# Audio tower block on one core: the first loads reordered and split, x in two parts, and three small steps moved between VectorE and GpSimd

## The chip, the cores and the metric

One core of one Trainium2 chip. The time is device microseconds (us) of one execution of the whole program, from its inputs in device memory to the output there. Engines: TensorE (PE, with its weight loads PEld), VectorE (DVE), ScalarE (ACT), GpSimd (POOL), SyncE (SP, whose queue issues most transfers).

## What is computed

An audio of 32 rows by 1024 samples is cut into patches of 16, which gives 32 batches of 64 tokens. Per token:

```
h = silu(x_cat @ W_h.T + b_h) @ W_o.T + b_o + x_cat @ W_r.T + b_r      # 16 samples -> 512 -> 256
h = h + attention(layernorm(h)) @ W_out.T + b_out                      # 16 heads of 16, Wq Wk Wv 16x16
h = h + real(ifft(fft(layernorm(h)) @ (w_real + i w_imag))) + bias     # 256 x 256 mix
```

The layernorms have no weights; eps is 1e-5. All is float32 at the ends.

## The kernel before

The 2048 tokens are T = 16 tiles of 128 tokens. The engines' programs are written out by hand, each with its own order and its own waits on semaphores; an engine never passes a waiting instruction.

**Start (to about 17 us).** SyncE issues twenty loads one after the other (`L254` to `L272`): all of x (`xs`, sixteen pieces of 64 bytes for each partition), the biases `bh`, `br`, `bo`, the identity, `wo_raw` (W_o, 512 KB), three small `wqk`, tables of the attention, W_out and the frequency weights and tables (`freq_loaded` counts four, the last is `sine`). ScalarE's queue loads W_h and W_r. x and the weights W_h, W_r with their biases are each split into three bfloat16 terms: place a term, subtract it, place the rest, twice over. ScalarE places x (`L316`), VectorE subtracts (`L597`) and does all of the weights (`L587`, `L592`). TensorE turns the stacks of terms (`turn_stacks`, `L844`, and `L860`), and W_o in `L850`; ScalarE makes the leading part `wo_hi` (`L328`), VectorE the rest `wo_lo` (`L625`). TensorE then mixes tile 0 (`mix`, `L887` to `L893`), only after all of W_o is split. The small products for the attention weights (`L910`, `L911`), and W_out turned (`L916`) stand between tile 0 and tile 1, and their copies on VectorE (`L646` to `L655`) before tile 2.

**Stage 1 (17 to 46 us), a loop over tiles 2 to 15.** For each tile TensorE makes the hidden layer (`hidden`, `L874`), ScalarE its silu twice (`L335`, `L338`), VectorE the remainder `hid_lo` (`L631`), TensorE `mix`, ScalarE copies h (`L342`), VectorE takes its statistics (`L660`). GpSimd meanwhile waits for the frequency weights, folds them (`L464` to `L480`), adds a bias to each h (`residual_bias`, `L505`), and makes rstd (`L489`) and the normalized x (`L525`). VectorE waits for the first rstd in `mean_shift(0)` (`L673`, at t = 7), then keeps on with the value weights, the remainders, and the inputs of the first scores.

**Stage 2 (46 to 147 us), steps i = -1 to 16.** Step i holds work of several tiles. On TensorE: turn the h2 of tile i-1 (`turn_side`, `L974`), turn maxima and x, scores of tile i+2, scores of tile i+1 less their maxima, frequency mix of tile i-1 (`mix_freq`), projection of tile i (`project`), query, and the weighted values (`weigh`, `L985`, `L990`). On VectorE: `divide` (`L758` to `L771`), `variance2(i-1)` (`L792`, `L794`, and `L798`, which adds eps), `split_x`, four row maxima (`L744`), `split_max` (`L751` a cast, `L753` a subtraction with both inputs in SBUF, both only 16 wide), `residual` (`L788`, which makes h2), `finish` (y, `L780`). On GpSimd, in this order: `place_same` (`L497`), `split_side` (`L532`), `split_on` (`L538`), `inv_std2` (`L511`, a power), `add_bias` (h2b, `L517`), `residual_bias` of tile 10 + i while that is below 16, so in steps 0 to 5 (`L505`, hb_all), and `normalize` of tile i+4, so up to step 11 (`L525`, xh). The next `turn_side` on TensorE waits for `residual`.

In step 0 VectorE also makes `mix_lo` (`L699`, 128 x 512), for which the first projection waits (`L1017`).

## Time and profile before

| what | value |
|---|---|
| median of 3 runs | 148.73 us (148.66 to 148.88) |
| the profiled execution | 149.01 us, span from first to last instruction 147.2 us |
| granted TensorE clock | 1.000 of full speed |
| 0 to 7.5 us | PE idle, DVE busy 2.69, ACT 3.15, POOL 2.63 |
| 7.5 to 17 us | PE 9.24 of 9.50, DVE 6.73, POOL 3.20 |
| 17 to 45 us | PE 27.55 of 28.00, DVE 21.81, ACT 19.69, POOL 21.19 |
| 72 to 90 us | PE 17.18 of 18.00, DVE 16.55, ACT 11.41, POOL 13.85 |
| 90 to 129 us | PE 38.59 of 39.00, DVE 35.44, ACT 25.68, POOL 26.32 |
| 129 to 147.2 us | PE 13.66 of 18.20, DVE 12.05, POOL 7.84 |

The busy times overlap within an engine where instructions are pipelined, so a busy engine is not necessarily at its limit; what ended each wait tells more. In the timelines a row is one instruction or a run of like ones, and the bracket at its end tells how long the engine was idle before it and what released it.

### The profile page before, as it was taken

Reading aid. Unit: us, or ns where it says so; the run is one execution under the profiler, and the core shown is the slowest. Engines: PE = TensorE matmul, PEld = TensorE weight load, DVE = VectorE, ACT = ScalarE, POOL = GpSimd, SP = SyncE. Lnnn points to the kernel's source line nnn. Section 1 sums busy time; section 2 is a strip of 40 time slices with the busy share of each in tenths; the row PEclk is TensorE's granted clock in tenths of the full one; section 3 lists DMA queues with packets and bytes.
Section 4 is the critical chain, followed back from the end, with each engine's and each line's share of the span. In section 5 each row is a group of like instructions: output and inputs, shape, how many; then the busy total and the mean of one; then the engine's idle time right before and its main releaser. Section 6 shows DMA issues by size and latency. Waiting matters only on the chain.

```text
span 147.2 us, 6094 instructions
## 1 busy us (share of the span) xinstructions
PE 131.7 (89%) x2434; PEld 113.2 (77%) x2434; DVE 117.8 (80%) x350; ACT 88.1 (60%) x248; POOL 89.5 (61%) x160
## 2 busy tenths in 40 slices
PE   0099899999999999999899999999999999999872
PEld 0098899999988877868678787897898887887641
DVE  0747964879977469899998989989989889889671
ACT  4478475747969475837558476486495594663310
POOL 6020999998230015879786786865776766673351
PEclk9999999999999999999999999999999999999999
DMA  4567000021000001102112012022131131121102
GB/s 63 161 162 254 4 0 0 0 25 17 2 0 4 0 9 20 18 25 33 46 19 58 32 26 52 8 58 47 13 60 43 14 58 40 18 53 42 33 10 71
DMA packets 24492, 5.89 MB, mean 40 GB/s; under 512 B 20368, under 2 KB 24208, under 8 KB 24464
## 3 DMA queue, kind: packets, MB, share of 16 engines
q1 hardware_dynamic: 24176, 5.40, 17.3%
q8 instruction: 19, 0.31, 0.9%
q10 hardware_dynamic: 288, 0.10, 0.3%
q14 instruction: 9, 0.07, 0.2%
HBM read 2.35 MB, written 2.10 MB: 30 GB/s over the span
## 4 chain that ended last, share of the span: by engine, by line
PE 57%; DVE 19%; issue 12%; POOL 4%; ACT 3%; DMA 2%; POOLq 0%; DVEq 0%
PE bank L946 9%; PE bank L932 6%; PE bank L887 6%; DVE rowmax L744 5%; PE bank L1007 3%; PE bank L985 3%; PE bank L891 3%; PE bank L974 3%; PE bank L990 2%; PE bank L1028 2%; DMA xs<-in_x 2%; PE bank L959 2%; DVE hid_lo L631 2%; PE bank L874 2%; PE bank L1041 2%
## 5 line engine op out<-in xcount | busy, mean ns | idle before, releaser
L744 DVE TENSOR_REDUCE rowmax<-bank 128x4 f32<-128x256 f32 x64 | 22.7, 418 | 5.6 <-ACT pT L371 5.3
L371 ACT ACTIVATE pT<-bank 128x256 f32<-128x256 f32 x64 | 19.4, 390 | 2.5 <-PE bank L959 2.5
L497 POOL TENSOR_SCALAR xblk<-xh,parity_sb 128x128 f32<-128x128 f32 x32 | 11.5, 371 | 14.3 <-PE bank L990 14.3
L946 PE MATMUL bank<-qT,xzT 32*128 32x64 f32 x512 | 17.9, 276 | 0.0
L946 PEld LDWEIGHTS bank<-qT,xzT 32*128 32x128 f32 x512 | 15.7, 186 | 2.7 <-issue 2.7
L631 DVE TENSOR_TENSOR hid_lo<-hidT,hid_hi 128x512 fp32r<-128x512 f32 x16 | 12.2, 761 | 5.6 <-ACT hidT L338 5.5
L366 ACT ACTIVATE maxT<-bank 128x128 fp32r<-128x128 f32 x16 | 4.4, 277 | 19.8 <-PE bank L968 19.8
L532 POOL TENSOR_TENSOR side_lo<-sideT,side_hi 128x256 fp32r<-128x256 f32 x14 | 10.2, 730 | 9.5 <-ACT sideT L381 9.5
L538 POOL TENSOR_TENSOR on_lo<-onT,on_hi 128x256 fp32r<-128x256 f32 x14 | 10.3, 735 | 7.2 <-ACT on_hi L385 7.0
L505 POOL TENSOR_TENSOR hb_all<-h_all,bout_bc 128x256 f32<-128x256 f32 x16 | 12.4, 789 | 0.0
L361 ACT ACTIVATE qT<-bank 128x256 f32<-128x256 f32 x16 | 6.2, 388 | 9.9 <-PE bank L1052 9.9
L356 ACT ACTIVATE xzT<-bank,parity_sb 128x256 f32<-128x256 f32 x28 | 12.0, 498 | 0.0
L517 POOL TENSOR_TENSOR h2b<-h,fbias_bc 128x256 f32<-128x256 f32 x16 | 11.7, 731 | 0.0
L990 PEld LDWEIGHTS bank<-pT,xblk 128*32 128x32 f32 x512 | 9.5, 110 | 2.8
L511 POOL TENSOR_TENSOR rstd<-ve,half_neg 128x1 f32<-128x1 f32 x16 | 8.9, 554 | 4.4 <-DVE ve L798 4.4
L932 PE MATMUL bank<-xzT,qT 32*64 32x128 f32 x512 | 11.5, 280 | 0.0
L887 PE MATMUL bank<-wo_hi,hid_hi 128*128 128x256 f32 x64 | 11.4, 300 | 0.0
L335 ACT ACTIVATE hid_hi<-bank 128x512 fp32r<-128x512 f32 x16 | 9.6, 601 | 2.7 <-PE bank L874 2.7
L342 ACT ACTIVATE h_all<-bank 128x256 f32<-128x256 f32 x16 | 6.2, 385 | 8.2 <-PE bank L893 8.2
L525 POOL TENSOR_SCALAR xh<-h_all,rstd,shift 128x256 f32<-128x256 f32 x16 | 9.6, 600 | 1.2 <-issue 0.5
L891 PE MATMUL bank<-wo_hi,hid_lo 128*128 128x256 f32 x64 | 10.3, 282 | 0.0
L985 PE MATMUL bank<-pT,pair_ones_sb 128*32 128x256 f32 x128 | 10.2, 391 | 0.0
(152 smaller groups left out, 388.5 us busy)
## 6 DMA issues: line engine op xcount, KB each, us to landing
out<-y SPq DMA_DIRECT2D x16, 128.0 KB, 1.7
xblk<-xh SPq DMA_DIRECT2D x32, 32.0 KB, 2.2
wo_raw<-in_W_o SPq DMA_DIRECT2D x1, 512.0 KB, 3.7
wout_raw<-in_W_out SPq DMA_DIRECT2D x1, 256.0 KB, 3.0
fr<-in_wr SPq DMA_DIRECT2D x1, 256.0 KB, 4.3
fi<-in_wi SPq DMA_DIRECT2D x1, 256.0 KB, 4.3
xs<-in_x SPq DMA_DIRECT2D x1, 128.0 KB, 3.3
minus_raw<-in_minus_rows SPq DMA_DIRECT2D x1, 128.0 KB, 2.2
```

The source lines that it names most:

```text
L356: nc.scalar.activation(xzT[t % 3][:, :, e, :], bank[X_BANK][:, 0:D].rearrange("p (g k) -> p g k", k=TOK), ACT.Copy, scale=parity[:, e:e + ...
L371: nc.scalar.activation(pT[:, j, :], bank[j][:, D:2 * D], ACT.Exp).then_inc(exp_done, 1)
L505: nc.gpsimd.tensor_tensor(hb_all[:, t, :], h_all[:, t, :], bout_bc[:], ALU.add).then_inc(hb_done, 1)
L517: nc.gpsimd.tensor_tensor(h2b[t % 2][:], h2[t % 2][:], fbias_bc[:], ALU.add).then_inc(h2b_done, 1)
L631: nc.vector.tensor_tensor(hid_lo[:, par, :], hidT[:, par, :], hid_hi[:, par, :].bitcast(F32), ALU.subtract).then_inc(lo_done, 1)
L744: nc.vector.tensor_reduce(rowmax[:, j, :], bank[j][:, 0:D].rearrange("p (h k) -> p h k", k=TOK), AX_X, ALU.max).then_inc(max_done, 1)
L887: pe.matmul(bank[MIX_BANK[par]][:, 0:D], hid_hi[:, par, c * P:(c + 1) * P], w[:, c, :], start=(c == 0 and w is wo_hi), stop=False)
L891: pe.matmul(bank[MIX_BANK[par]][:, 0:D], hid_lo[:, par, c * P:(c + 1) * P], wo_hi[:, c, :], start=False, stop=False)
L932: last = pe.matmul(bank[j][TOK * b:TOK * b + TOK, half * P:(half + 1) * P], qT[t % 3][rows32, half, TOK * b:TOK * b + TOK], xzT[t % 3][row ...
L946: pe.matmul(bank[j][:, at0:at0 + TOK], xzT[t % 3][rows32, 2 * half + b, :, :].rearrange("p e k -> p (e k)"), qT[t % 3][rows32, half, TOK * ...
L985: pe.matmul(bank[PV_BANK][32 * j:32 * j + 32, D:2 * D], pair_ones[:], pT[:, j, :], start=True, stop=True)
L990: last = pe.matmul(bank[PV_BANK][32 * j:32 * j + 32, cols], xblk[t % 2][:, b, half * P + 32 * j:half * P + 32 * j + 32], pT[:, j, cols], s ...
```

## The change

- **Loads.** SyncE first loads four tiles of x (`HEAD` = 4), then b_h, W_o, W_r, b_r, b_o, the three small weights, the other twelve tiles of x, and the rest as before. The identity goes to ScalarE's queue behind W_h. b_h, W_h, W_r, the biases, and the two parts of x have semaphores of their own.
- **First four tiles of x.** ScalarE places them as before, GpSimd subtracts. VectorE does only W_h (four of the six columns of weights) before TensorE turns it; GpSimd then does W_r's terms.
- **Last twelve tiles of x.** GpSimd places and subtracts them after that; TensorE turns them at t = 2 and t = 3 of the loop, VectorE copies them at t = 3 and t = 4.
- **Tile 0.** W_o is turned in two halves; VectorE copies the leading part of the first, ScalarE that of the second. `mix(0)` takes its products in the order in which the operands arrive, with W_r's product last.
- **Later places in stage 1.** W_out is turned at t = 4, copied at t = 4 (VectorE); the small copies at t = 3, the score split at t = 5, the value weights at t = 5 instead of t = 4. Zeros for `xblk` and `max_terms` are set by VectorE.
- **Stage 2.** `mix_lo` is made by GpSimd in step 0 (waited for by `mix_freq(0)`, no longer by `project(0)`). eps is added by GpSimd ahead of the power, in `inv_std2`, for all 16 tiles; VectorE's `L798` goes.

```diff
+HEAD = 4
...
-        WO_BANK = (2, 3, 4, 5)
+        WO_BANK = (2, 3)
+        WR_BANK = 7
...
-            sp.dma_start(xs[:], x_tok).then_inc(x_loaded, 16)
-            sp.dma_start(bh[:], a["b_h"].rearrange("(p c) -> p c", p=P)).then_inc(b_loaded, 16)
-            sp.dma_start(br[:], a["b_r"].rearrange("(p c) -> p c", p=P)).then_inc(b_loaded, 16)
-            sp.dma_start(bo[:], a["b_o"].rearrange("(p c) -> p c", p=P)).then_inc(b_loaded, 16)
-            sp.dma_start(ident[:], a["identity"]).then_inc(ident_loaded, 16)
+            sp.dma_start(xs[:, 0:HEAD, :], x_tok[:, 0:HEAD, :]).then_inc(x_loaded, 16)
+            sp.dma_start(bh[:], a["b_h"].rearrange("(p c) -> p c", p=P)).then_inc(bh_loaded, 16)
             sp.dma_start(wo_raw[:], a["W_o"].rearrange("(c p) i -> p c i", p=P)).then_inc(wo_loaded, 16)
+            sp.dma_start(wf_raw[:, NC:, :], a["W_r"].rearrange("(p c) f -> p c f", p=P)).then_inc(wr_loaded, 16)
+            sp.dma_start(br[:], a["b_r"].rearrange("(p c) -> p c", p=P)).then_inc(br_loaded, 16)
+            sp.dma_start(bo[:], a["b_o"].rearrange("(p c) -> p c", p=P)).then_inc(br_loaded, 16)
             for i, name in enumerate(("Wq", "Wk", "Wv")):
-                sp.dma_start(wqk[:, i, :], a[name]).then_inc(att_loaded, 16)
+                sp.dma_start(wqk[:, i, :], a[name]).then_inc(wqk_loaded, 16)
+            sp.dma_start(xs[:, HEAD:, :], x_tok[:, HEAD:, :]).then_inc(x_late_loaded, 16)
...
-            sp.wait_ge(const_set, 8)
+            sp.wait_ge(zeros_set, 2)
...
-            act.dma_start(wf_raw[:, 0:NC, :], a["W_h"].rearrange("(p c) f -> p c f", p=P)).then_inc(w_loaded, 16)
-            act.dma_start(wf_raw[:, NC:, :], a["W_r"].rearrange("(p c) f -> p c f", p=P)).then_inc(w_loaded, 16)
-
+            act.dma_start(wf_raw[:, 0:NC, :], a["W_h"].rearrange("(p c) f -> p c f", p=P)).then_inc(wh_loaded, 16)
+            act.dma_start(ident[:], a["identity"]).then_inc(ident_loaded, 16)
...
-                nc.scalar.activation(x_slots[:, :, X_SLOTS[part], 0:PATCH],
-                                     src[:].unsqueeze(2).to_broadcast([P, T, n, PATCH]), ACT.Copy).then_inc(x_placed, 1)
-
+                nc.scalar.activation(x_slots[:, 0:HEAD, X_SLOTS[part], 0:PATCH],
+                                     src[:, 0:HEAD, :].unsqueeze(2).to_broadcast([P, HEAD, n, PATCH]),
+                                     ACT.Copy).then_inc(x_placed, 1)
...
+            act.wait_ge(x_turned, 1)
             for g in range(2):
-                act.wait_ge(x_turned, g + 1)
-                nc.scalar.activation(x_termsT[:, g * HID:(g + 1) * HID], bank16[6 + g][:, 0:HID],
+                nc.scalar.activation(x_termsT[:, g * D:(g + 1) * D], bank16[6][:, g * D:(g + 1) * D],
                                      ACT.Copy).then_inc(x_copied, 1)
...
-                if at(t, 0):
-                    wo_leading((2, 3))
+                if at(t, 1):
+                    act.wait_ge(wo_turned, 2)
+                    nc.scalar.activation(wo_hi[:, 2:4, :].rearrange("p c n -> p (c n)"), bank[WO_BANK[1]][:],
+                                         ACT.Copy).then_inc(wo_copied, 1)
...
-            wo_leading((0, 1))
...
             nc.gpsimd.memset(half_neg[:], -0.5).then_inc(const_set, 1)
             nc.gpsimd.memset(w_terms[:, :, STACK:P], 0.0).then_inc(const_set, 1)
-            nc.gpsimd.memset(x_terms[:, :, STACK:P], 0.0).then_inc(const_set, 1)
             nc.gpsimd.memset(x_slots[:, :, 0:3, PATCH], 1.0).then_inc(const_set, 1)
             nc.gpsimd.memset(x_slots[:, :, 3:TERMS, PATCH], 0.0).then_inc(const_set, 1)
-            for i in range(2):
-                nc.gpsimd.memset(xblk[i][:], 0.0).then_inc(const_set, 1)
-            nc.gpsimd.memset(max_terms[:].bitcast(F32), 0.0).then_inc(const_set, 1)
+            nc.gpsimd.memset(x_terms[:, :, STACK:P], 0.0).then_inc(const_set, 1)
...
+            def x_remainder(part, src):
+                pool.wait_ge(x_placed, part + 1)
+                nc.gpsimd.tensor_tensor(x_rest[part][:], src[:, 0:HEAD, :], x_slots[:, 0:HEAD, X_SLOTS[part].start, 0:PATCH],
+                                        ALU.subtract).then_inc(x_rest_set, 1)
+
+            def place_wr(part, src):
+                n = len(range(*W_SLOTS[part].indices(TERMS)))
+                nc.gpsimd.tensor_copy(w_slots[:, NC:, W_SLOTS[part], :],
+                                      src[:, NC:, :].unsqueeze(2).to_broadcast([P, HALF, n, TERM])).then_inc(wr_placed, 1)
...
+            def place_late(part, src):
+                n = X_SLOTS[part].stop - X_SLOTS[part].start
+                nc.gpsimd.tensor_copy(x_slots[:, HEAD:, X_SLOTS[part], 0:PATCH],
+                                      src.unsqueeze(2).to_broadcast([P, T - HEAD, n, PATCH])).then_inc(x_late_placed, 1)
...
+            def late_remainder(part, src):
+                pool.wait_ge(x_late_placed, part + 1)
...
+
+            x_remainder(0, xs)
             pool.wait_ge(ident_loaded, 16)
             nc.gpsimd.tensor_copy(ident16[:], ident[:]).then_inc(ident16_set, 1)
-
-
-            pool.wait_ge(att_loaded, 112)
+            pool.wait_ge(x_rest_set, 1)
+            x_remainder(1, x_rest[0])
+
+            pool.wait_ge(wr_set, 4)
+            place_wr(0, wb)
+            wr_remainder(0, wb)
+            place_wr(1, wb_rest[0])
+            wr_remainder(1, wb_rest[0])
+            place_wr(2, wb_rest[1])
...
+            pool.wait_ge(wqk_loaded, 48)
...
+            pool.wait_ge(x_late_loaded, 16)
+            place_late(0, xs[:, HEAD:, :])
+            late_remainder(0, xs[:, HEAD:, :])
+            place_late(1, x_late_rest[0][:])
+            late_remainder(1, x_late_rest[0][:])
+            place_late(2, x_late_rest[1][:])
...
-            pool.wait_ge(const_set, 8)
+            pool.wait_ge(zeros_set, 2)
...
             def inv_std2(t):
-                pool.wait_ge(ve2_done, t + 1)
+                pool.wait_ge(mv2_done, t + 1)
+                nc.gpsimd.tensor_scalar(ve2[:], mv2[:, 1:2], EPS, None, ALU.add).then_inc(ve2_done, 1)
                 if t >= 2:
                     pool.wait_ge(y_set, t - 1)
+                pool.wait_ge(ve2_done, t + 1)
                 nc.gpsimd.tensor_tensor(rstd2[t % 2][:], ve2[:], half_neg[:, 0:1], ALU.pow).then_inc(rstd2_done, 1)
...
+            def split_mix_weights():
+                pool.wait_ge(mix_led, 1)
+                pool.wait_ge(mix_kept, 1)
+                nc.gpsimd.tensor_tensor(mix_lo[:], mix_whole[:], mix_hi[:].bitcast(F32), ALU.subtract).then_inc(mix_split, 1)
...
             def step(i):
                 if i + 2 < T:
                     place_same(i + 2)
+                if i == 0:
+                    split_mix_weights()
...
+            for i in range(2):
+                nc.vector.memset(xblk[i][:], 0.0).then_inc(zeros_set, 1)
+            nc.vector.memset(max_terms[:].bitcast(F32), 0.0).then_inc(zeros_set, 1)
...
+            dve.wait_ge(wh_loaded, 16)
+            nc.vector.tensor_copy(wb[:, 0:NC, 0:PATCH], wf_raw[:, 0:NC, 0:PATCH]).then_inc(wh_set, 1)
+            nc.vector.tensor_reduce(wb[:, 0:NC, PATCH], wf_raw[:, 0:NC, PATCH:], AX_X, ALU.add).then_inc(wh_set, 1)
+            dve.wait_ge(bh_loaded, 16)
+            dve.wait_ge(wh_set, 2)
+            nc.vector.tensor_tensor(wb[:, 0:NC, PATCH], wb[:, 0:NC, PATCH], bh[:], ALU.add).then_inc(wh_set, 1)
+            dve.wait_ge(wh_set, 3)
+            place_wh(0, wb)
+            wh_remainder(0, wb)
+            place_wh(1, wb_rest[0])
+            wh_remainder(1, wb_rest[0])
+            place_wh(2, wb_rest[1])
+
+            dve.wait_ge(wr_loaded, 16)
+            nc.vector.tensor_copy(wb[:, NC:, 0:PATCH], wf_raw[:, NC:, 0:PATCH]).then_inc(wr_set, 1)
+            nc.vector.tensor_reduce(wb[:, NC:, PATCH], wf_raw[:, NC:, PATCH:], AX_X, ALU.add).then_inc(wr_set, 1)
+            dve.wait_ge(w_turned, 1)
+            nc.vector.tensor_copy(w_termsT[:, 0:HID], bank16[0][:, 0:HID]).then_inc(w_copied, 1)
+            dve.wait_ge(br_loaded, 32)
+            nc.vector.tensor_tensor(br[:], br[:], bo[:], ALU.add).then_inc(wr_set, 1)
+            dve.wait_ge(wr_set, 3)
+            nc.vector.tensor_tensor(wb[:, NC:, PATCH], wb[:, NC:, PATCH], br[:], ALU.add).then_inc(wr_set, 1)
...
+            dve.wait_ge(wo_turned, 1)
+            nc.vector.tensor_copy(wo_hi[:, 0:2, :].rearrange("p c n -> p (c n)"), bank[WO_BANK[0]][:]).then_inc(wo_led, 1)
...
+            remainder(0, 0)
+            for g in range(2):
+                wo_remainder(g)
+            dve.wait_ge(wr_turned, 1)
             nc.vector.tensor_copy(wr_termsT[:].rearrange("f (p c) -> f c p", c=HALF),
-                                  bank16[1][:, 0:D].rearrange("f (c p) -> f c p", c=HALF)).then_inc(w_copied, 1)
-            wo_remainder(range(NC))
-            remainder(0, 0)
+                                  bank16[WR_BANK][:, 0:D].rearrange("f (c p) -> f c p", c=HALF)).then_inc(wr_copied, 1)
             remainder(1, 1)
...
+            def copy_small():
+                dve.wait_ge(att_loaded, 64)
+                dve.wait_ge(small_done, 2)
...
+            def copy_wout():
+                for c in range(HALF):
...
+            def copy_late(g):
+                dve.wait_ge(x_late_turned, g + 1)
...
             for t in range(3, T):
+                if t == 3:
+                    copy_late(0)
                 remainder(t, t % 2)
+                if t == 3:
+                    copy_small()
+                if t == 4:
+                    copy_late(1)
                 h_stats(t - 2)
+                if t == 4:
+                    copy_wout()
+                if t == 5:
+                    split_score()
...
                 nc.vector.bn_stats(stats2[:], h2[t % 2][:]).then_inc(stats2_done, 1)
                 dve.wait_ge(stats2_done, t + 1)
+                if t >= 1:
+                    dve.wait_ge(ve2_done, t)
                 nc.vector.bn_aggr(mv2[:], stats2[:]).then_inc(mv2_done, 1)
-                dve.wait_ge(mv2_done, t + 1)
-                if t >= 1:
-                    dve.wait_ge(rstd2_done, t)
-                nc.vector.tensor_scalar(ve2[:], mv2[:, 1:2], EPS, None, ALU.add).then_inc(ve2_done, 1)
...
-                if i == 0:
-                    split_mix_weights()
...
-            dve.wait_ge(const_set, 8)
+            dve.wait_ge(zeros_set, 3)
...
+                if at(t, 0):
+                    pe.wait_ge(x_copied, 2)
+                    pe.wait_ge(wo_led, 1)
+                    leading(t, par, wo_hi, (0, 1))
+                    pe.wait_ge(wo_copied, 1)
+                    leading(t, par, wo_hi, (2, 3))
+                    pe.wait_ge(lo_done, 1)
+                    remaining(t, par)
+                    pe.wait_ge(wo_split, 2)
+                    leading(t, par, wo_lo, range(NC))
+                    pe.wait_ge(wr_copied, 1)
...
             hidden(0, 0)
-            turn_wo((2, 3))
-            pe.wait_ge(w_copied, 2)
+            pe.wait_ge(ident_loaded, 16)
+            pe.wait_ge(wo_loaded, 16)
+            turn_wo(0)
             hidden(1, 1)
-            pe.wait_ge(x_copied, 2)
-            turn_stacks(8, 8, 7)
-            mix(0, 0)
-            hidden(2, 0)
-
+            turn_wo(1)
             pe.wait_ge(reps_set, 2)
             pe.matmul(bank[4][:, 0:P], wrep[:, 0, :], wrep[:, 1, :], start=True, stop=True).then_inc(small_done, 1)
             pe.matmul(bank[4][:, P:2 * P], erep[:], wrep[:, 2, :], start=True, stop=True).then_inc(small_done, 1)
-
-            pe.wait_ge(wout_loaded, 16)
+            pe.wait_ge(wr_placed, 3)
             for c in range(HALF):
-                for k in range(HALF):
-                    last = pe.transpose(bank[2 + c][:, k * P:(k + 1) * P], wout_raw[:, k, c * P:(c + 1) * P], ident[:])
-                last.then_inc(wout_turned, 1)
+                last = pe.transpose(bank16[WR_BANK][:, c * P:(c + 1) * P], w_terms[:, NC + c, :], ident16[:])
+            last.then_inc(wr_turned, 1)
+            mix(0, 0)
+            hidden(2, 0)
             mix(1, 1)
...
+                if t == 0:
+                    pe.wait_ge(mix_split, 1)
...
-                    pe.wait_ge(mixw_copied, 1)
+                    pe.wait_ge(mix_kept, 1)
...
+                if t == 2:
+                    pe.wait_ge(x_late_placed, 3)
+                    turn_stacks(HEAD, HEAD, 7, x_late_turned)
+                if t == 3:
+                    pe.wait_ge(x_late_copied, 1)
+                    turn_stacks(2 * HEAD, 2 * HEAD, 7, x_late_turned)
+                if t == 4:
+                    turn_wout()
+                if t == 7:
+                    pe.wait_ge(x_late_copied, 2)
...
-                if t == 4:
+                if t == 5:
+                    pe.wait_ge(wout_copied, HALF)
                     value_weights()
```

## Rows read from the trace of the kernel before

**Rows 1.** The page: busy time, share of the span and instructions of each engine.
```profile
PE 131.7 (89%) x2434; PEld 113.2 (77%) x2434; DVE 117.8 (80%) x350; ACT 88.1 (60%) x248; POOL 89.5 (61%) x160
```

**Rows 2.** TensorE's instructions in order of time: start us, us, work, [idle before].
```profile
7.56 0.58 PE L860 MATMUL bank<-ident,w_terms 128*128 128x128 bf16 x4 [7.56 <-DVE w_terms L587]
...
17.18 0.40 PE L874 MATMUL bank<-x_termsT,w_termsT 128*128 128x128 bf16 x4 [0.39 <-DVE woutT L655]
```

**Rows 3.** SyncE's queue in order of time: start us, us to issue, transfer.
```profile
1.22 1.51 SPq L255 DMA_DIRECT2D bh<-in_b_h  x1
...
10.49 0.43 SPq L271 DMA_DIRECT2D sine_sb<-in_sine  x1
```

**Rows 4.** GpSimd in order of time, 14 to 28 us.
```profile
14.88 0.74 POOL L464 TENSOR_TENSOR rows<-fr 128x256 f32<-128x256 f32 x1 [4.17 <-DMA sine_sb<-in_sine]
...
19.64 0.39 POOL L472 COPY rows<-fi 1x256 f32<-1x256 f32 x1
...
20.11 0.46 POOL L475 TENSOR_TENSOR cols<-rows 128x127 f32<-128x127 f32 x1
...
20.51 0.19 POOL L476 COPY cols<-rows 128x1 f32<-128x1 f32 x1
...
27.33 1.41 POOL L489 TENSOR_TENSOR rstd<-ve,half_neg 128x4 f32<-128x4 f32 x1
```

**Rows 5.** VectorE in order of time, 28 to 33 us.
```profile
28.78 0.69 DVE L673 SCALAR_TENSOR_TENSOR shift<-mv,rstd 128x4 f32<-128x4 f32 x1 [0.60 <-POOL rstd L489]
...
32.35 0.69 DVE L631 TENSOR_TENSOR hid_lo<-hidT,hid_hi 128x512 fp32r<-128x512 f32 x1 [0.75 <-ACT hidT L338]
```

**Rows 6.** Chain of waits, 15 to 58 us: start us, us, the work.
```profile
40.72 0.43 DVE x_lo L711
```

**Rows 7.** All engines in order of time, 80 to 89 us (step 4; last row step 5).
```profile
80.01 0.74 POOL L538 TENSOR_TENSOR on_lo<-onT,on_hi 128x256 fp32r<-128x256 f32 x1 [0.57 <-ACT on_hi L385]
...
81.23 0.73 POOL L517 TENSOR_TENSOR h2b<-h,fbias_bc 128x256 f32<-128x256 f32 x1
...
81.86 0.17 DVE L751 CAST max_terms<-rowmax 128x16 fp32r<-128x16 f32 x1
...
81.92 0.73 POOL L505 TENSOR_TENSOR hb_all<-h_all,bout_bc 128x256 f32<-128x256 f32 x1
...
82.07 0.61 DVE L753 TENSOR_TENSOR max_terms<-rowmax,max_terms 128x16 fp32r<-128x16 f32 x1
...
82.61 0.41 DVE L788 TENSOR_TENSOR h<-bank,hb_all 128x256 f32<-128x256 f32 x1
...
88.52 0.41 DVE L788 TENSOR_TENSOR h<-bank,hb_all 128x256 f32<-128x256 f32 x1
```

**Rows 8.** VectorE and GpSimd at the end of step 2, in order of time.
```profile
69.70 0.45 DVE L751 CAST max_terms<-rowmax 128x16 fp32r<-128x16 f32 x1
...
70.08 0.73 POOL L505 TENSOR_TENSOR hb_all<-h_all,bout_bc 128x256 f32<-128x256 f32 x1
...
70.18 0.66 DVE L753 TENSOR_TENSOR max_terms<-rowmax,max_terms 128x16 fp32r<-128x16 f32 x1
```

**Rows 9.** VectorE and GpSimd in steps 6 and 9, in order of time.
```profile
93.78 0.55 POOL L525 TENSOR_SCALAR xh<-h_all,rstd,shift 128x256 f32<-128x256 f32 x1
...
93.90 0.45 DVE L753 TENSOR_TENSOR max_terms<-rowmax,max_terms 128x16 fp32r<-128x16 f32 x1
...
110.93 0.55 POOL L525 TENSOR_SCALAR xh<-h_all,rstd,shift 128x256 f32<-128x256 f32 x1
...
111.01 0.19 DVE L753 TENSOR_TENSOR max_terms<-rowmax,max_terms 128x16 fp32r<-128x16 f32 x1
```

**Rows 10.** TensorE's `turn_side` of steps 5 and 12, in order of time.
```profile
89.08 0.41 PE L974 MATMUL bank<-ident,h 128*128 128x128 f32 x2 [0.27 <-DVE h L788]
...
128.88 0.44 PE L974 MATMUL bank<-ident,h 128*128 128x128 f32 x2
```

**Rows 11.** GpSimd at step 0, in order of time.
```profile
55.95 0.73 POOL L538 TENSOR_TENSOR on_lo<-onT,on_hi 128x256 fp32r<-128x256 f32 x1 [1.36 <-ACT on_hi L385]
```

185 lines of the change are left out of this document (83 added, 102 removed).

## The prediction

> **What bounds the kernel now.** I read the page first: PE is busy for 89% of the span, DVE for 80%, POOL for 61% [rows 1]. So three engines are near enough to a limit that a share decides nothing, and I went by stage. Start: PE does nothing before 7.56 us, where it has waited for the last term of the weights, and its loop begins with hidden(3) at 17.18 [rows 2]. SP's queue shows why the inputs are late: b_h took 1.51 us to issue, against 0.43 for others, behind the many small pieces of x; the last frequency table was issued only at 10.49 [rows 3]. GpSimd waited for that table until 14.88, then worked without a gap worth the name to its first rstd at 27.33 [rows 4]. VectorE waits for this rstd: its shift starts at 28.78 and takes 0.69 instead of some 0.15, as it stands behind GpSimd. After the value weights it idles 0.75, then runs from 32.35 [rows 5] as the chain itself to 40.72 [rows 6]. So GpSimd and then VectorE, not PE, set the later part of stage 1.
>
> Stage 2 has the important pattern. In step 4 GpSimd goes on_lo, power, h2b, hb_all back to back. VectorE's `L753`, a subtraction of 16 columns, starts at 82.07 and lasts 0.61; it ends at 82.68, just behind the end of hb_all (81.92 + 0.73 = 82.65). h2 follows at 82.61, and everything on PE follows h2 [rows 7]. Step 2 shows the pattern for a GpSimd that is a little later: the cast `L751` is held to 70.15, and `L753`, at 70.18, finds hb_all begun at 70.08 and is held to 70.84 [rows 8]. So in steps 1 to 5 the period (88.52 - 82.61 = 5.91 for h2 [rows 7]) is the time of GpSimd's chain, though the chain of waits names VectorE and "issue". In steps 6 and on there is no hb_all. In step 6 `L753`, 0.12 behind the start of xh, is held to 94.35; in step 9, only 0.08 behind it, it slips in and takes 0.19 [rows 9]. From step 5 to step 12, `turn_side` moves from 89.08 to 128.88, seven periods of 5.69 [rows 10], close to what PE needs.
>
> **The change, part by part.** The sum is made on the profiled execution (149.01); I carry its differences over to the median, 148.73, which lies 0.28 lower.
>
> *Loads.* A quarter of x leaves a quarter of b_h's stall of 1.51 - 0.43 = 1.08: 0.27. b_h and what follows comes about 0.8 earlier, and W_o goes third instead of sixth. Behind the other twelve tiles the next issue pays the stall back (0.75 x 1.08 = 0.81), and there is one more load (W_r joins, the late x joins, the identity leaves), 0.47. The last table thus moves by -0.81 + 0.81 + 0.47 = +0.47 at most; if the stall isn't proportional, by nothing. I take +0.3: GpSimd's rows start near 15.2. The late x on GpSimd is five operations; at 0.46 for 127 columns [rows 4] and 192 to 576 columns each, some 3.3 us, and the W_r part some 2. They end near 14, in the wait before 14.88, so they are hidden; if that cover failed, stage 1 would be later by the overrun.
>
> *PE's start.* With b_h and W_h early and x of four tiles, its first transpose comes near 5.2 instead of 7.56. PE then waits for GpSimd's small copies, which stand behind the W_r terms (near 9.8), so the loop gains less. Into the loop move turns of x and W_out of 1.0 us together. I put PE ahead by 1.5 us at t = 7. There it stops: `turn_x(0)` at t = 8 needs GpSimd's xh, and VectorE needs GpSimd's rstd. The extra copies on VectorE at t = 3 to 5 lie before that wait. Behind it only the idle 0.75 before 32.35 [rows 5] can go, with its 0.06 of hand-over, as silu(9) is now early: 0.81. Less the 0.3 of the table: **-0.5**. Bounds: 0 (the table is later, or a copy stalls PE) and -1.5 (all of PE's lead).
>
> *Mix of tile 0 by arrival* costs nothing of its own: the same thirteen products. Its gain is inside PE's start.
>
> *mix_lo on GpSimd.* 512 columns at twice 0.73 is 1.4 us; GpSimd idles 1.36 before on_lo at step 0 [rows 11]. Zero; without that gap it would be 1.4 in one step.
>
> *eps on GpSimd.* VectorE loses a tiny operation in each step. In step 4 it stood idle before the maxima anyway, so I count no gain. GpSimd gains one ahead of its power. The nearest row is the copy of one column: 0.19, and it frees its successor after some 0.18. The power must then wait for it; a wait of GpSimd for itself shows as 0.08 (19.64 + 0.39 to 20.11) [rows 4]. So the GpSimd chain is 0.26 longer; bounds 0.15 (no wait seen) and 0.45. Queued behind it are h2b, hb_all, xh. In step 4, h2b would end at 82.22, the cast be held to it, and `L753` come 0.10 behind hb_all's start, as in step 2: held, and h2 0.26 later. Five steps, 1 to 5: 5 x 0.26 = **+1.3** (0.75 to 2.2).
>
> *Steps 6 to 12.* In step 6 h2b ends at 94.05, the cast at 94.08, `L753` starts at 94.11, that is 0.07 behind xh at 94.04. In step 9 0.08 was enough to slip in [rows 9]. Then it ends at 94.29 instead of 94.35. Steps where it was not held lose 0.1 or so, those where it was held gain 0.06: **0** (-0.2 to +0.3).
>
> At that point a rule speaks against the row. The Trainium skill ("SBUF — State Buffer", Who interferes with whom) says that of a VectorE instruction with two SBUF inputs and a GpSimd instruction that reads SBUF, whichever issues first keeps the shared port to its end. By that rule xh, 0.07 earlier, wins, and the sum is that of the second rival below.
>
> *Tail.* In the last two tiles GpSimd waits for VectorE's eps. Added 0.26, removed an operation of VectorE: between 0 and 0.26 each, I take 0.1 each: **+0.2**.
>
> Sum: -0.5 + 1.3 + 0 + 0.2 = +1.0. 148.73 + 1.0 = 149.7.
>
> **The rivals.** *(1) Faster: the lead of the start survives and eps is hidden.* If the small addition is done while the port is VectorE's, or `L753` gets the port between h2b and hb_all, steps 1 to 5 cost nothing. That leaves 148.73 - 0.5 = 148.2, and down to 147.2 if PE's whole 1.5 is kept. It decides where h2 in step 4 comes less than 0.1 later after `turn_side`. For it: the start has much to win. Against it: step 2's row, and that GpSimd, not PE, is ahead of VectorE at t = 7. *(2) `L753` loses to xh.* Then in step 6 it ends at 94.04 + 0.55 + 0.03 = 94.62 instead of 94.35: +0.27 in four steps that were held before, and some +0.4 in three that weren't: +2.3, in all 152.0. For it: hb_all held a subtraction 0.10 behind. Against it: the 0.08 of step 9. *(3) Both ends meet.* The full 1.5 of the start and +1.3 +0.2 of stage 2: 148.7, no change. The gain of the start would have to pass the wait for rstd, for which the freq loads must land 0.5 us earlier, not later.
>
> That mix_lo or the W_r terms hold up PE I count into (2)'s side: both have cover, and both would be some tenths.
>
> **How the numbers follow.** A measurement of this kernel can tell about 0.2%, 0.3 us, from no change. Forecast 0.45 (its own range 149.1 to 150.5), rival (1) 0.25, (2) 0.20, (3) 0.10. Slower: 0.45 + 0.20 = 0.65; faster 0.25; same 0.10. The range takes in all of the forecast, (3), the upper half of (1) and most of (2): 148.0 to 152.0.
>
> **What would show it.** PE's first transpose near 5.2 and hidden(3) near 14.7. GpSimd's rows at 15.0 to 15.4, its first rstd at 27.4 to 27.8. VectorE's hid_lo of tile 9 near 31.8 with no idle time before it, the first maximum near 45.5 instead of 46.05. In steps 3 to 5 periods of h2 of 6.17 instead of 5.91, with `L753` ending just behind hb_all. In steps 6 to 12 `L753` of 0.19, periods near 5.7. The forecast is wrong if the periods of steps 3 to 5 are under 6.0, if `L753` in step 7 takes over 0.4, or if the first maximum comes before 45.0 or after 46.1.

## The result and the profile after the change

The changed kernel takes 152.42 us (median of 4 runs, 152.15 to 154.79), the kernel before 148.81 (4 runs) beside it: ratio 1.0221, 95% interval 1.0194 to 1.0248. It is slower, as forecast, but by 3.6 us instead of 1.0, and outside the range (148.0 to 152.0). The fourth run, at 154.79, lies apart from the other three (152.15 to 152.46) and isn't in the ratio. The profiled execution took 152.15 us, with a span of 150.4 against 147.2.

The head of the page of the changed kernel, to set beside [rows 1]:

```profile
span 150.4 us, 6108 instructions
...
PE 131.8 (88%) x2434; PEld 112.9 (75%) x2434; DVE 119.6 (80%) x336; ACT 86.4 (57%) x245; POOL 99.7 (66%) x186
```

GpSimd has gained 16 small operations and the late x, VectorE has lost 16: its share did not fall, since some of the work it kept takes longer (the held casts below).

The span splits at the sums h of tiles 0, 5, 12, 13 and 15 on VectorE. First of the kernel before, then of the changed one (start us, us, the work, [idle before]):

```profile
58.34 0.42 DVE L788 TENSOR_TENSOR h<-bank,hb_all 128x256 f32<-128x256 f32 x1
...
128.24 0.42 DVE L788 TENSOR_TENSOR h<-bank,hb_all 128x256 f32<-128x256 f32 x1
133.63 0.42 DVE L788 TENSOR_TENSOR h<-bank,hb_all 128x256 f32<-128x256 f32 x1
...
141.83 0.42 DVE L788 TENSOR_TENSOR h<-bank,hb_all 128x256 f32<-128x256 f32 x1 [0.58 <-PE bank L1021]
```

```profile
56.75 0.42 DVE L859 TENSOR_TENSOR h<-bank,hb_all 128x256 f32<-128x256 f32 x1
...
88.85 0.41 DVE L859 TENSOR_TENSOR h<-bank,hb_all 128x256 f32<-128x256 f32 x1
...
130.79 0.42 DVE L859 TENSOR_TENSOR h<-bank,hb_all 128x256 f32<-128x256 f32 x1
136.36 0.42 DVE L859 TENSOR_TENSOR h<-bank,hb_all 128x256 f32<-128x256 f32 x1
...
144.57 0.42 DVE L859 TENSOR_TENSOR h<-bank,hb_all 128x256 f32<-128x256 f32 x1 [0.77 <-PE bank L1100]
```

With the h of tile 5 at 88.52 before [rows 7]: the start is 1.59 shorter (forecast -0.5), tiles 0 to 5 take 32.10 instead of 30.18, +1.92 (forecast +1.3), tiles 5 to 12 take 41.94 instead of 39.72, +2.22 (forecast 0), and from there to the end 19.61 instead of 18.96, +0.65 (forecast +0.2). The sum is +3.2, the difference of the spans. From here on "step i" is the period that ends with the h of tile i.

Step 4 of the changed kernel, GpSimd and VectorE in order of time, beside [rows 7]:

```profile
79.27 0.75 POOL L591 TENSOR_TENSOR on_lo<-onT,on_hi 128x256 fp32r<-128x256 f32 x1 [0.57 <-ACT on_hi L388]
...
80.11 0.23 POOL L555 TENSOR_SCALAR ve<-mv 128x1 f32<-128x1 f32 x1
80.48 0.58 POOL L559 TENSOR_TENSOR rstd<-ve,half_neg 128x1 f32<-128x1 f32 x1
81.03 0.73 POOL L565 TENSOR_TENSOR h2b<-h,fbias_bc 128x256 f32<-128x256 f32 x1
81.12 0.67 DVE L822 CAST max_terms<-rowmax 128x16 fp32r<-128x16 f32 x1
81.72 0.73 POOL L551 TENSOR_TENSOR hb_all<-h_all,bout_bc 128x256 f32<-128x256 f32 x1
81.83 0.65 DVE L824 TENSOR_TENSOR max_terms<-rowmax,max_terms 128x16 fp32r<-128x16 f32 x1
82.40 0.41 DVE L859 TENSOR_TENSOR h<-bank,hb_all 128x256 f32<-128x256 f32 x1
```

From the start of on_lo to that of the power is 1.21 us, against 0.69 before (80.01 to 80.70): the edit puts **0.52** in between, where I forecast 0.26. The operation itself takes 0.23; it starts 0.09 behind the end of on_lo, and the power 0.14 behind its own end. Before, the power started 0.05 ahead of the end of on_lo. All that follows is as drawn: the cast is held to the end of h2b, `L824` finds hb_all begun and is held, h comes that much later. The next h is at 88.85, a period of 6.45 instead of 5.91.

Only steps 1, 4 and 5 look like this (6.44, 6.46 and 6.45 instead of 5.98, 5.93 and 5.91). In step 2 both small operations come ahead of h2b:

```profile
68.41 0.17 DVE L822 CAST max_terms<-rowmax 128x16 fp32r<-128x16 f32 x1
68.62 0.17 DVE L824 TENSOR_TENSOR max_terms<-rowmax,max_terms 128x16 fp32r<-128x16 f32 x1
...
68.83 0.74 POOL L565 TENSOR_TENSOR h2b<-h,fbias_bc 128x256 f32<-128x256 f32 x1
...
70.24 0.56 POOL L573 TENSOR_SCALAR xh<-h_all,rstd,shift 128x256 f32<-128x256 f32 x1
```

So h comes at once, at 68.73, and the step takes 5.54. But h2b, hb_all and xh then stand behind h: xh starts 1.51 behind it, where it started 0.04 behind it before (70.80 behind 70.76). Step 3 takes 7.21. The two together take 12.75 instead of 12.36, less than twice the price.

Step 7, where there is no hb_all:

```profile
98.17 0.74 POOL L591 TENSOR_TENSOR on_lo<-onT,on_hi 128x256 fp32r<-128x256 f32 x1 [0.57 <-ACT on_hi L388]
...
99.92 0.73 POOL L565 TENSOR_TENSOR h2b<-h,fbias_bc 128x256 f32<-128x256 f32 x1
100.02 0.66 DVE L822 CAST max_terms<-rowmax 128x16 fp32r<-128x16 f32 x1
100.64 0.55 POOL L573 TENSOR_SCALAR xh<-h_all,rstd,shift 128x256 f32<-128x256 f32 x1
100.72 0.20 DVE L824 TENSOR_TENSOR max_terms<-rowmax,max_terms 128x16 fp32r<-128x16 f32 x1
100.83 0.41 DVE L859 TENSOR_TENSOR h<-bank,hb_all 128x256 f32<-128x256 f32 x1
```

Here `L824` slips in 0.08 behind xh, as forecast. But h2b now begins 0.10 ahead of the cast, so the cast is held and lasts 0.66, and GpSimd's chain sets these steps too: seven periods of 5.98 to 6.00 instead of 5.49 to 5.86.

The last output sum and what it waited for, before and then changed:

```profile
143.45 0.18 DVE L794 BATCH_NORM_AGGREGATE mv<-stats 128x2 f32<-128x6 f32 x1
...
144.54 0.48 DVE L780 SCALAR_TENSOR_TENSOR y<-bank,rstd,h2b 128x256 f32<-128x256 f32 x1 [0.72 <-POOL rstd L511]
```

```profile
146.40 0.18 DVE L867 BATCH_NORM_AGGREGATE mv<-stats 128x2 f32<-128x6 f32 x1
...
147.70 0.48 DVE L851 SCALAR_TENSOR_TENSOR y<-bank,rstd,h2b 128x256 f32<-128x256 f32 x1 [1.12 <-POOL rstd L559]
```

It stands 1.30 behind the statistics instead of 1.09: here the move of the addition costs 0.21.

The start, by its main rows:

```profile
13.62 0.39 PE L934 MATMUL bank<-x_termsT,w_termsT 128*128 128x128 bf16 x4
...
14.68 0.74 POOL L510 TENSOR_TENSOR rows<-fr 128x256 f32<-128x256 f32 x1 [1.58 <-DMA sine_sb<-in_sine]
...
26.92 1.03 POOL L535 TENSOR_TENSOR rstd<-ve,half_neg 128x4 f32<-128x4 f32 x1
...
44.47 1.42 DVE L815 TENSOR_REDUCE rowmax<-bank 128x4 f32<-128x256 f32 x4 [0.17 <-PE bank L1009]
```

TensorE begins at 5.07 (forecast 5.2) and hidden(3) at 13.62 (forecast 14.7; 17.18 before). The last table was issued at 10.21 instead of 10.49 and GpSimd began at 14.68, not near 15.2. The first rstd is 0.41 earlier and the first maximum stands at 44.47 instead of 46.05, ahead of the 45.0 that the prediction named as a sign of being wrong. In step 0 the remainder of the mix took 1.28 us on GpSimd and ended at 54.25, just ahead of on_lo at 54.36.

### The profile page after: what moved, and what is told of

Its sections match the earlier page's. It is cut to its first block, busy times and chain, and to the rows that moved or that the text cites. A ratio compares the mean times of both kernels' runs of the same rounds, so it can differ in the third digit from the quotient of the medians.

```text
span 150.4 us, 6108 instructions
## 1 busy us (share of the span) xinstructions
PE 131.8 (88%) x2434; PEld 112.9 (75%) x2434; DVE 119.6 (80%) x336; ACT 86.4 (57%) x245; POOL 99.7 (66%) x186
## 4 chain that ended last, share of the span: by engine, by line
DVE 26%; POOL 20%; PE 17%; ACT 14%; issue 12%; SPq 6%; DMA 3%; POOLq 1%; DVEq 0%
DVE rowmax L815 7%; DVE max_terms L822 4%; POOL hb_all L551 4%; PE bank L1023 3%; ACT xzT L359 3%; ACT pT L374 3%; DMA sine_sb<-in_sine 3%; DVE h L859 3%; PE bank L1051 3%; PE bank L1009 3%; DVE hid_lo L690 2%; PE bank L940 2%; POOL h2b L565 2%; ACT on_hi L388 1%; POOL rstd L535 1%
## 5 line engine op out<-in xcount | busy, mean ns | idle before, releaser
L543 POOL TENSOR_SCALAR xblk<-xh,parity_sb 128x128 f32<-128x128 f32 x32 | 12.0, 390 | 11.5 <-PE bank L1067 10.5
L1023 PEld LDWEIGHTS bank<-qT,xzT 32*128 32x128 f32 x512 | 15.7, 186 | 2.7 <-issue 2.7
L690 DVE TENSOR_TENSOR hid_lo<-hidT,hid_hi 128x512 fp32r<-128x512 f32 x16 | 12.5, 778 | 4.4 <-ACT hidT L342 4.4
L1051 PE MATMUL bank<-ident,h 128*128 128x128 f32 x32 | 6.7, 290 | 6.4 <-DVE h L859 6.4
L565 POOL TENSOR_TENSOR h2b<-h,fbias_bc 128x256 f32<-128x256 f32 x16 | 11.7, 732 | 0.0
L940 PE MATMUL bank<-wo_lo,hid_hi 128*128 128x256 f32 x64 | 10.2, 281 | 0.0
```

Source lines behind the costliest of these rows:

```text
L543: last = nc.gpsimd.tensor_scalar(xblk[t % 2][:, b, :].rearrange("p (g e d) -> p g e d", e=2, d=HD)[:, :, b, :], xh[t % 2][:].rearrange("p ...
L565: nc.gpsimd.tensor_tensor(h2b[t % 2][:], h2[t % 2][:], fbias_bc[:], ALU.add).then_inc(h2b_done, 1)
L690: nc.vector.tensor_tensor(hid_lo[:, par, :], hidT[:, par, :], hid_hi[:, par, :].bitcast(F32), ALU.subtract).then_inc(lo_done, 1)
L940: pe.matmul(bank[MIX_BANK[par]][:, 0:D], hid_hi[:, par, c * P:(c + 1) * P], w[:, c, :], start=(c == 0 and w is wo_hi), stop=False)
L1023: pe.matmul(bank[j][:, at0:at0 + TOK], xzT[t % 3][rows32, 2 * half + b, :, :].rearrange("p e k -> p (e k)"), qT[t % 3][rows32, half, TOK * ...
L1051: last = pe.transpose(bank[SIDE_BANK][:, D + half * P:D + (half + 1) * P], h2[t % 2][:, half * P:(half + 1) * P], ident[:])
```

## The experiments

The theory A after this: the eps addition costs 0.52 us in a chain that sets every step, some 4.3 us from the h of tile 0 to that of tile 13, and the rest of the change is a gain. The rivals are told with each run. "Before" below is the kernel before on the same chip in the same batch: 148.89, 149.03, 149.11 and 149.24 in four batches.

**1. Only the eps addition put back.** The changed kernel with:

```diff
 def inv_std2(t):
-    pool.wait_ge(mv2_done, t + 1)
-    nc.gpsimd.tensor_scalar(ve2[:], mv2[:, 1:2], EPS, None, ALU.add).then_inc(ve2_done, 1)
...
+    nc.vector.tensor_scalar(ve2[:], mv2[:, 1:2], EPS, None, ALU.add).then_inc(ve2_done, 1)
```

> The changed kernel with the addition of eps back on VectorE, all else as changed. Theory A (the addition is what made stage 2 longer: GpSimd's chain from on_lo to the power grew from 0.69 to 1.21 us, in every step): h2 of tile 0 to h2 of tile 13 takes 75.3 us again instead of 79.6, the tail 0.4 less, and the start keeps its 1.6: 147.1 us. Rival B (the later place of mix_lo, or the port shared by VectorE and GpSimd in general, made it longer): at least a third of the 4.1 us stays, 148.5 us or more.

148.19 us (147.59 to 149.2, 12 runs), ratio to the kernel before 0.996 [0.9934, 0.9986]. So this one operation carries the whole loss: 152.42 to 148.19 is 4.2 us, and the loss was 3.6. In the profile the steps are back (h of tile 0 to h of tile 13: 74.91 us, against 79.61 changed and 75.29 before), and from there to the end it takes 13.5 instead of 14.0. The time still missed theory A's 147.1, as the start's gain is absent in this profile: the first maximum is at 45.98, not at 44.47. Part 9 is about that.

**2. The eps addition alone, on the kernel before.**

> The kernel before with only the addition of eps on GpSimd. Theory A: stage 2 grows by 4.1 us and the tail by 0.5 as in the changed kernel, without the start's gain: 153.3 us, with periods of h2 of 6.0 in steps 7 to 12 and 6.45 in steps 4 and 5. Rival B: under 151 us, as the other moves carry part of it.

154.02 us, ratio 1.0346 [1.0313, 1.0379]; periods 6.44, 5.54, 7.20, 6.45, 6.42, then seven of 5.97 to 6.00, as in the changed kernel within 0.03. The loss needs nothing else of the change. Of the 5.2 us in the profile 4.2 lie between the h of tile 0 and that of tile 13 (79.53 against 75.29), 0.4 behind it, and 0.6 ahead of it, where nothing was edited (part 9).

**3. The same operation, issued ahead of on_lo,** where GpSimd waits 0.57 for ScalarE.

```diff
...
+if i >= 1:
+    add_eps2(i - 1)
 if i < WHOLE_ON:
     split_on(i)
```

> The changed kernel with the addition of eps still on GpSimd, but issued ahead of on_lo, where GpSimd idled 0.57 us for on_hi, and not behind it. Theory A (it is the place in GpSimd's chain that costs): on_lo at the same distance behind turn_side (2.77) and power 0.69 behind on_lo: as the kernel with eps on VectorE, 147.1 to 147.6 us, in steps 1 and 2, where GpSimd has no gap, up to 0.5 each more. Rival C (a GpSimd tensor_scalar of one column disturbs VectorE through the shared port wherever it stands): 150 us or more.

148.67 us, ratio 0.9999 [0.9968, 1.0029]. GpSimd of this kernel in step 8:

```profile
101.93 0.23 POOL L563 TENSOR_SCALAR ve<-mv 128x1 f32<-128x1 f32 x1 [0.24 <-DVE mv L873]
102.27 0.74 POOL L595 TENSOR_TENSOR on_lo<-onT,on_hi 128x256 fp32r<-128x256 f32 x1
102.97 0.58 POOL L557 TENSOR_TENSOR rstd<-ve,half_neg 128x1 f32<-128x1 f32 x1
```

From on_lo to the power it is 0.70 again, and steps 6 to 12 take 5.49 to 5.63. The operation is as long as it was; what it cost was its place. Rival C (150 or more) is out, but theory A's 147.1 to 147.6 was missed too. From the h of tile 0 to that of tile 13 it takes 75.41, 0.5 more than in run 1, and from the last h to the end 6.3 us against 5.3 there: in the last step the h2b that GpSimd did while it waited for VectorE now stands behind the addition, between it and the power. This profile has the early start (44.71), which hides most of that.

**4. One more operation of a column between eps and the power.**

> The changed kernel with one more operation on one column (times 1) between the addition of eps and the power on GpSimd, waited for in the same way. Theory A' (the two small operations of VectorE are held because GpSimd's h2b has begun 0.11 us ahead of the first; with another 0.37 h2b begins after it, and both slip in ahead of h2b, as in step 2 of the changed kernel, where h2 came 5.54 us after the last): periods of steps 7 to 12 fall from 6.00 to about 5.6 to 5.8, and the time by 1 to 3 us although work was added: about 150 us. Rival D (GpSimd's chain as such sets the period): each period grows by 0.37, in all some 4.5 us: 157 us.

155.61 us, ratio 1.0453 [1.0401, 1.0505]. Neither: steps 6 to 12 take 6.06, only 0.07 more.

```profile
107.63 0.17 DVE L826 CAST max_terms<-rowmax 128x16 fp32r<-128x16 f32 x1
107.83 0.73 POOL L569 TENSOR_TENSOR h2b<-h,fbias_bc 128x256 f32<-128x256 f32 x1
107.84 0.76 DVE L828 TENSOR_TENSOR max_terms<-rowmax,max_terms 128x16 fp32r<-128x16 f32 x1
108.52 0.41 DVE L863 TENSOR_TENSOR h<-bank,hb_all 128x256 f32<-128x256 f32 x1
```

The cast slips in before h2b (by 0.20), but the subtraction comes 0.01 behind it and is held to its end. What is held has changed, and so the cost of a delay is not proportional: the first 0.52 gave 0.32 per step here, a further 0.30 (on_lo to the power 1.51) gave 0.07. Most of the 3.2 us against the changed kernel lies outside: h of tile 0 is 1.4 later (the two outcomes of part 9), and 0.8 comes behind the h of tile 13. A' failed narrowly: in step 2, where the subtraction came 0.02 ahead of h2b, it was not held, and the step took 5.96.

**5. The same addition as a sum of two columns.**

```diff
-nc.gpsimd.tensor_scalar(ve2[:], mv2[:, 1:2], EPS, None, ALU.add)
+nc.gpsimd.tensor_tensor(ve2[:], mv2[:, 1:2], eps_col[:], ALU.add)
```

> The changed kernel with the eps addition on GpSimd as an addition of two columns (variance and a column that holds eps) in place of an addition of a constant. Theory: the 0.52 us that the edit puts between on_lo and the power is one dispatch of a dependent GpSimd operation, whatever its form: 0.5 to 0.55 again, 152.0 to 152.8. Rival: the constant form carries a gap of 0.14 us behind it that the other form does not: 0.35 to 0.4 between, steps 5.8 to 5.85 instead of 6.0, 150.0 to 150.8.

151.13 us (150.49 to 151.38), ratio 1.0134 [1.0099, 1.0169]; periods of 6.25 and 6.24 in steps 4 and 5 and 5.77 to 5.80 in 6 to 12. The time lies between the two forecasts. GpSimd:

```profile
104.62 0.74 POOL L596 TENSOR_TENSOR on_lo<-onT,on_hi 128x256 fp32r<-128x256 f32 x1 [0.57 <-ACT on_hi L390]
105.32 0.19 POOL L560 TENSOR_TENSOR ve<-mv,eps_col 128x1 f32<-128x1 f32 x1
105.65 0.56 POOL L564 TENSOR_TENSOR rstd<-ve,half_neg 128x1 f32<-128x1 f32 x1
```

The rival's price is nearly right (1.03 from on_lo to the power, so 0.34), its reason is not: the gap of 0.14 behind the operation is still there. What went is the gap ahead of it (it starts 0.04 before on_lo's end, not 0.09 behind) and 0.04 of its own time. Steps 4 and 5 again grow by the price (6.24 against 5.92). Steps 6 to 12 grow by 0.11 each, so the loss there by price is 0.11 for 0.34, 0.32 for 0.52 and 0.39 for 0.82 (run 4).

**6. The remainder of the mix back on VectorE as well.**

> The changed kernel with the eps addition and the remainder of the mix both back on VectorE: the reordered loads, the early parts on VectorE, the late x parts on GpSimd and the order of arrival stay. With the eps addition alone put back the time was 148.19 us. Theory: the remainder of the mix is worth nothing, since on_lo(0) waits for GpSimd's xh work either way: 148.2, within 147.9 to 148.6, and the first output of tile 0 within 0.3 us of where it was. Rival: VectorE's extra operation delays the mix of tile 1 and with it the second softmax: 148.9 or more.

148.18 us, ratio 0.9948 [0.9921, 0.9975], against 148.19 with it on GpSimd. Where it runs makes no difference that these runs can tell (their intervals are some 0.4 us wide to each side).

**7. The residual and bias sum early in steps 1 to 5.** If GpSimd's chain sets those steps, hb_all should leave it for GpSimd's idle time ahead of side_lo.

```diff
+if i >= 1 and EARLY + i < T:
+    residual_bias(EARLY + i)
 if 1 <= i <= WHOLE_SIDE:
     split_side(i - 1)
...
-if EARLY + i < T:
-    residual_bias(EARLY + i)
+if i == 0:
+    residual_bias(EARLY)
```

> The changed kernel with the eps addition back on VectorE; in the steps 1 to 5 the residual and bias sum of GpSimd is issued ahead of the split of the x side, where GpSimd has 0.75 us of idle time. Theory: in those steps the subtraction waits behind that sum into the next VectorE operation, so the steps shorten from 5.93 to about 5.6 us, 1.2 to 1.5 us in all: 146.7 to 147.1. Rival: what ends the step is VectorE's chain of normalisation and the sum only moves the wait: steps 5.9, 148.2.

147.10 us (146.56 to 147.72), ratio 0.9877 [0.9848, 0.9906], 1.1 less than without. Steps 1 to 6 take 5.98, 5.98, 6.12, 5.61, 5.86, 5.49. Step 4 of this kernel:

```profile
79.86 0.73 POOL L563 TENSOR_TENSOR h2b<-h,fbias_bc 128x256 f32<-128x256 f32 x1
80.49 0.17 DVE L822 CAST max_terms<-rowmax 128x16 fp32r<-128x16 f32 x1
80.58 0.57 POOL L571 TENSOR_SCALAR xh<-h_all,rstd,shift 128x256 f32<-128x256 f32 x1
80.70 0.17 DVE L824 TENSOR_TENSOR max_terms<-rowmax,max_terms 128x16 fp32r<-128x16 f32 x1
80.81 0.42 DVE L859 TENSOR_TENSOR h<-bank,hb_all 128x256 f32<-128x256 f32 x1
```

Neither small operation waits. In the kernel before, `L753` lasted 0.61 at this place [rows 7]. But the number was hit in part by luck: steps 1 to 5 became 0.68 us shorter than in run 1 (29.55 against 30.23), not 1.2 to 1.5, and this profile has the early start (44.85 against 45.98). The same move on the kernel before:

> The kernel before with the residual and bias sums of the steps 1 to 5 issued ahead of the split of the x side, nothing else changed. Theory: the gain belongs to the steps, not to the changed start, so it is the same 1.0 us as on the changed kernel (147.10 against 148.19): 147.9, within 147.6 to 148.2, with steps 3 to 5 of 5.6 instead of 5.92 us. Rival: it needs the changed start, since in the kernel before GpSimd's idle time ahead of the split is taken by other work: 148.6 to 149.0.

148.47 us (147.84 to 149.18), ratio 0.9952 [0.9931, 0.9974]; steps 1 to 6 take 5.98, 5.97, 6.13, 5.60, 5.87, 5.78. A gain of 0.6, less than the theory's 1.0 and more than the rival's 0 to 0.4. In the profile steps 1 to 5 take 29.55, the same as with the changed start, and 0.63 less than the 30.18 before; another 0.26 went in steps 6 to 12, which were not edited. So the gain belongs to the steps, at some 0.65 us, and what the changed kernel showed above that is not of this edit. Why it is less than forecast, the rows show: with hb_all gone, xh is what the subtraction meets. In step 5 of both profiles the subtraction started 0.12 or 0.13 behind xh and was held (0.43 and 0.45 us), and the step took 5.86 and 5.87; in step 4 it started 0.11 and 0.12 behind xh, was not held, and the step took 5.60 and 5.61. In steps 6 to 12 of the nine profiles with eps on VectorE the same tells the longer steps (held, 5.75 to 5.88) from the shorter ones (not held, 5.49 to 5.64), with two exceptions in run 6's kernel (5.71 and 5.85, not held).

**8. The frequency tables ahead of W_out.**

> The changed kernel with the eps addition back on VectorE, and the loads of W_out and of the output bias moved behind the four loads of the frequency tables on their queue. Theory: GpSimd's chain of the RMS rows starts when the sine tables land (14.6 to 15.0 us so far), so it starts up to 0.9 us earlier here, VectorE's 2.67 us of waiting ahead of the shift shrinks by as much, the first row maximum comes at 45.0 to 45.4 instead of 45.9, and the time is 147.3 to 147.9. Rival: the tables' landing goes by the traffic that all queues share, not by the place in this queue: the chain starts at 14.6 to 15.0 again and the time is 148.2.

GpSimd's rows start at 13.43 instead of 14.95 (run 1), more than forecast, and yet the median is 148.53. The twelve runs fall apart: three at 146.48 to 146.58, seven at 148.42 to 148.62, two above 149.2. Neither forecast had two times in it. With run 7's edit added:

> The changed kernel with the eps addition back on VectorE, the residual and bias sums of the steps 1 to 5 early (147.10 us with these two), and W_out and the output bias loaded behind the frequency tables, which alone made GpSimd's chain start 1.4 us earlier and gave three runs at 146.5 and nine at 148.4 to 149.4. Theory: the two add: 145.3 in some runs, 147.3 in most, with a median of 145.3 to 147.3. Rival: the gain of the tables shows only where the first softmax waits for GpSimd; in this program the start waits for a Silu in all runs, and the time is 147.1 or more in every one.

Three runs at 145.87 to 146.33, four at 148.1 to 148.66: two groups as in the theory, each 0.6 to 1.4 us later. In both profiles (149.44 and 148.24, both of the longer kind) the steps take nearly what they took in runs 1 and 7 (74.93 and 74.42 us from the h of tile 0 to that of tile 13, against 74.91 and 74.07), and tile 0 is late, with the first maximum at 46.83 and 46.16, although GpSimd began early.

**9. What divides the runs.** The rows that differ between profiles of nearly the same start are TensorE's. Four products of 128x256 in the first mix, of the changed kernel and then of the kernel of run 1:

```profile
9.91 0.72 PE L940 MATMUL bank<-wo_hi,hid_hi 128*128 128x256 f32 x4
```

```profile
10.78 1.20 PE L940 MATMUL bank<-wo_hi,hid_hi 128*128 128x256 f32 x4
```

The granted clock of both stretches is 1.00 in the profile, so the clock column does not tell them apart; the durations do. With the time of the first maximum beside it:

| profile | first mix, us for four | first maximum |
|---|---|---|
| changed kernel | 0.72 | 44.47 |
| eps ahead of on_lo | 0.72 | 44.71 |
| hb_all early | 0.73 | 44.85 |
| start alone (run 6) | 0.72 | 45.07 |
| one more operation | 1.20 | 45.88 |
| eps back | 1.20 | 45.98 |
| two columns | 1.20 | 46.15 |
| tables first and hb_all early | 1.20, and so the second | 46.16 |
| tables first | 1.20, and so the second | 46.83 |

So the -1.59 of the changed kernel's profile is one of two outcomes; in the other the start gains nothing (46.05 before). The start of the kernel before varies too, by less: in its own profile and in that of its variant in part 7 the first mix took 0.72 us (first maximum at 46.05 and 46.01), in that of run 2 it took 0.88 (46.62). No one kernel was profiled in both outcomes; that the same rows divide the runs of a single kernel is inferred from this table. Run 3's times fit it, nine at 148.4 to 148.71 and two at 150.04 and 150.37. The Trainium skill ("TensorE: Matmul & The Clock Gate", What's actually happening) says that the engine's clock is held at its lower level, 1.2 GHz, until it has been busy, and that the moment differs from run to run. That fits the two kinds of rows. Hence the next try: eight products of zeros from 1.2 us on and two more before the first hidden product, results overwritten.

```diff
+pe.wait_ge(busy_set, 1)
+idle_work(8, 512)
 pe.wait_ge(ident16_set, 1)
...
+idle_work(2, 256)
 def hidden(t, par):
```

> The changed kernel with the eps addition back on VectorE (148.19 us, 147.59 to 149.2), and TensorE kept busy from about 1.2 us: eight matmuls of 512 columns of zeros ahead of the first transposes and two of 256 columns between the transposes of the weights and the first hidden product. Their results are overwritten. Theory: how long TensorE's matmuls last at the start decides the time of a run: where four products of 128x256 last 0.72 us from the first mix on, the first row maximum stood at 44.5 to 45.1, where they last 1.20 us until 13.7 us or 15.9 us, at 45.9 to 46.8. With the engine busy from 1.2 us the first mix runs at 0.72 in every run, the first row maximum is at 44.4 to 45.0, and all runs lie within 146.5 to 147.7, median 147.2. Rival: the spread has another source (the landing of the loads), and the added matmuls only delay the first transposes by up to 0.5 us: 148.2 to 148.7 with the same spread.

> The three together: the eps addition on VectorE, the residual and bias sums of the steps 1 to 5 early, the tables ahead of W_out, and TensorE kept busy from about 1.2 us. Without the last the seven runs fell into two groups, 145.87 to 146.33 and 148.1 to 148.66. Theory: the upper group is that of a late rise of TensorE's clock, so it goes: all runs within 145.4 to 146.4, median 145.9. Rival: two groups again, a median of 147 to 148.

The first gave 148.08 us (147.75 to 148.68), the second 146.91 (146.17 to 147.59). TensorE in the profile of the first, then of the second:

```profile
1.17 3.59 PE L927 MATMUL bank<-busy 128*128 128x512 bf16 x8 [1.17 <-DVE busy L640]
...
5.84 0.63 PE L927 MATMUL bank<-busy 128*128 128x256 bf16 x2
...
10.77 1.20 PE L950 MATMUL bank<-wo_hi,hid_hi 128*128 128x256 f32 x4
```

```profile
5.85 0.38 PE L929 MATMUL bank<-busy 128*128 128x256 bf16 x2
...
10.48 0.73 PE L952 MATMUL bank<-wo_hi,hid_hi 128*128 128x256 f32 x4
```

The eight products take 3.59 and 3.60 us, so one of 512 columns 0.45, or 1.1 columns a nanosecond: near the lower level of 1.2, though the granted clock reads 1.00 here too. The work up to 5.9 us is the same in both. In the second the engine is faster from there on, and the first maximum stands at 44.12; in the first it stays slow until 13.7 us, busy for 11.7 of the 12.5 us from 1.0 to 13.5, with the first maximum at 45.88. So the link between these rows and the start holds in both, and the landing of the tables doesn't give it: they came early where the first maximum was latest (13.43 and 46.83). But the remedy did not do what I forecast: being busy from 1.2 us does not bring the rise in every run, so what the Trainium skill says there does not by itself give the moment here. The first profile is of the slowest of its six runs; the other five (147.75 to 148.17) have none. For both kernels the rival's number is the nearer one. The second kernel's runs still form two groups (146.17 to 146.45, 147.38 to 147.59), and here the mean granted clock does differ, 0.993 to 1.000 against 0.984 to 0.985, which the groups of the other kernels do not show. These two groups may have another source. What decides the moment stays open.

Faster than both kernels are run 7's version, 147.10 us, and the one with all edits, 146.91 (ratio 0.9841 [0.9809, 0.9874]); the intervals of the two overlap. The shortest single times, 145.87 to 146.33, came from the version with the tables first and hb_all early, in three of its seven runs.

## Why the prediction was wrong

- **The step that failed is the price of the eps addition: "So the GpSimd chain is 0.26 longer; bounds 0.15 (no wait seen) and 0.45".** It measured 0.52, outside its own bounds, and 0.34 in the cheapest form (run 5). I took 0.18 for the operation and 0.08 for the wait. The rows show 0.23, a gap of 0.14 behind it where the power needs its result, 0.09 ahead of it, and the 0.05 by which the power had started before the end of on_lo. I had read both numbers off copies in the start [rows 4]; this operation was put between two of which the second did not wait for the first.
- **Steps 1 to 5: "+1.3" was +1.92.** Steps 1, 4 and 5 followed the drawn mechanism (cast held to h2b, subtraction held to hb_all; run 7 shows by removal that hb_all was in the way) and grew by 0.46, 0.53 and 0.54, the price at its right size. Steps 2 and 3 did not: together +0.39, since in step 2 both small operations went ahead of h2b. Five times 0.52 would have been 2.6.
- **Steps 6 to 12: "0" became +2.22, the largest part of the miss, and it comes from the same price.** The drawing was right: the cast held to the end of h2b, the subtraction 0.08 behind xh and not held. The same drawing with 0.52 in place of 0.26 gives, as an estimate from the rows of before, +0.21 in each of the four steps where the subtraction had been held (in step 7 it ends at 100.31 instead of 100.10) and +0.46 in each of the other three (in step 9 at 111.66 instead of 111.20), +2.2 in all. With 0.34 (run 5) these steps measured +0.8. The second rival (the subtraction loses to xh) did not occur, though its sum, 152.0, is nearest to the result; that is luck.
- **Against the Trainium skill's rule** ("SBUF — State Buffer", Who interferes with whom: who issues first keeps the shared port) I set the row in which 0.08 behind xh was no loss. That row repeated in steps 6 to 11 (step 12 has no xh). But 0.00 to 0.01 behind h2b (run 4) and 0.10 to 0.16 behind hb_all the same subtraction was held in every profile. Beside xh it slipped in at every distance up to 0.10, was held in some steps and not in others at 0.11 to 0.13 (held at 0.12 in [rows 9], not held at 0.12 in run 7's rows above), and was held at 0.14 (one row). So the rule agrees with all rows but those in the first 0.13 us beside xh, and the prediction's 0.07 there was on the safe side.
- **Stage 1: "-0.5", bounds 0 and -1.5.** -1.6 in the profile, 0 in other profiles of the same start. My reason, the 0.81 of idle time less a later table, was wrong in its second half (b_h took 0.50 to issue, so 1.01 was saved and not 0.81, and the pay-back behind the late x was 0.27, 0.70 against 0.43, and not 0.81; so the table came earlier) and blind to what goes with the two outcomes, the time of TensorE's products (part 9). Over the runs the change without the eps move is worth 0.7 to 0.9: 148.19 against 148.89 and 148.18 against 149.03, each with some 0.4 us to either side; not all of that need be the start, as run 1's profile has 0.4 of it in the steps. The idle 0.75 ahead of hid_lo of tile 9 did go (it starts at 30.72 without a wait here, and behind 0.16 in run 1's profile).
- **The remainder of the mix: 0.** Right, as far as the runs can tell (run 6).
- **The tail: +0.2** was +0.65: 0.18 in the step from tile 12 to 13, and behind the last h 0.21 twice, once each for tiles 14 and 15 (the rows above). I had taken 0.1 each, with 0.26 as the bound.

## What to carry to other kernels

Price an operation that is inserted between two that follow each other at once by the distance between their starts, not by its own duration: here 0.23 us of work cost 0.52, and nearly nothing in the steps when it was issued one place earlier, in an idle gap (though there it cost 1.0 us in the tail). When a chain is delayed, redraw every small operation beside it for the whole range of the delay; what is held changes, and the loss per step is not proportional: 0.11, 0.32 and 0.39 us for 0.34, 0.52 and 0.82. Before a gain at the start is believed from one profile, compare the durations of like matmuls in several: the start here had two outcomes, with the first maximum at 44.5 to 45.1 or at 45.9 to 46.8.

## What was not expected of the hardware

- One column added to a constant on GpSimd takes 0.23 us and starts 0.09 behind its predecessor's end; added to another column it takes 0.19 and starts 0.04 before that end. Either way the power that needs it starts 0.14 behind its end.
- A subtraction on VectorE that starts 0.01 us behind GpSimd's h2b is held to its end (0.76 instead of 0.17), one that starts 0.08 behind xh takes 0.20, and one that starts 0.11 to 0.13 behind xh takes 0.17 in some steps and 0.43 to 0.46 in others, of one and the same kernel.
- TensorE's products took 1.20 instead of 0.72 us for four until 13.7 us, or some 15.7, in some profiles while the granted clock read 1.00, in one (run 9's first) after 12 us of almost unbroken work.
